# Weighing values on all four quarters of the array, with the output in two banks

## What is computed

```python
pos = jnp.arange(seq_len)
seg = pos // SEGMENT_LENGTH                      # 64
local = seg[None, :] == seg[:, None]
diff = jnp.abs(pos[None, :] - pos[:, None])
dil = (diff > 0) & (diff % 4 == 0) & (diff <= 256)
scores = jnp.einsum('bqhd,bkhd->bhqk', q, k) * scaling + mask[None, None]
attn = jax.nn.softmax(scores, axis=-1)
out = jnp.einsum('bhqk,bkhd->bqhd', attn, v).reshape(B, S, H * Dh)
return out @ w_o
```

## Time and profile before

| | before |
|---|---|
| device time, median of 3 | 471.31 us |
| span of the profiled execution | 468.8 us |
| PE busy | 444.4 us, 95% |
| DVE busy | 394.0 us, 84% |
| ACT busy | 333.3 us, 71% |
| POOL busy | 296.6 us, 63% |
| chain that ended last | PE 59%, POOL 9%, DMA 8%, DVE 8%, ACT 7% |

### The profile page before, as it was taken

How to read it: one execution, slowest core, us unless ns; L and a number is a source line. 1 busy time by engine, 2 the same in 40 slices (tenths; PEclk the granted TensorE clock), 3 DMA queues, 4 the chain that set the end, 5 groups by cost and what they waited for, 6 DMA issues and landing times.

```text
span 468.8 us, 17264 instructions
## 1 busy us (share of the span) xinstructions
PE 444.4 (95%) x6440; PEld 350.0 (75%) x6440; DVE 394.0 (84%) x1344; ACT 333.3 (71%) x975; POOL 296.6 (63%) x491
## 2 busy tenths in 40 slices
PE   7997899999999999999999999998987989999996
PEld 6685688888888888788887778887744757558775
DVE  6885798987888899889887698995899989998775
ACT  3686768868877877886786678695566579987533
POOL 4321488677666858667865588564669897674322
PEclk9999899999999999999999999999999999999999
DMA  7577852346335445344455565364000000000003
GB/s 224 183 246 209 247 142 52 73 99 133 80 74 112 76 79 105 76 85 94 98 108 124 112 124 108 75 125 91 1 1 0 0 2 1 1 0 2 1 0 91
DMA packets 136099, 40.53 MB, mean 86 GB/s; under 512 B 104977, under 2 KB 131025, under 8 KB 136017
## 3 DMA queue, kind: packets, MB, share of 16 engines
q1 hardware_dynamic: 135440, 38.38, 35.7%
q10 hardware_dynamic: 576, 1.05, 0.6%
HBM read 29.44 MB, written 9.96 MB: 84 GB/s over the span
## 4 chain that ended last, share of the span: by engine, by line
PE 59%; POOL 9%; DMA 8%; DVE 8%; ACT 7%; SPq 4%; issue 3%; ACTq 0%; POOLq 0%; DVEq 0%
PE psum L422 10%; PE psum L464 10%; PE psum L484 5%; PE psum L1186 5%; DMA w_rows_dram<-st 4%; PE psum L498 4%; PE psum L495 4%; PE psum L403 4%; PE psum L510 4%; PE psum L1181 3%; PE psum L405 3%; PE psum L404 3%; DMA st<-w_rows_dram 2%; POOL area L1827 2%; ACT pband L569 2%
## 5 line engine op out<-in xcount | busy, mean ns | idle before, releaser
L948 POOL TENSOR_SCALAR pband<-pband,fac 128x192 f32<-128x192 f32 x256 | 103.9, 424 | 80.6 <-DVE fac L771 80.4
L569 ACT ACTIVATE pband<-pband,st 128x192 f32<-128x192 f32 x256 | 113.1, 447 | 1.0 <-DVE st L719 1.0
L719 DVE CUSTOM_DVE_ANT_0 pband<-psum,band_mask 128x192 f32<-128x192 f32 x256 | 76.1, 353 | 0.1
L422 PE MATMUL psum<-keys,q_class 64*64 64x192 f32 (+2 forms) x1536 | 66.2, 274 | 0.0
L464 PEld LDWEIGHTS psum<-ident,pband 128*128 128x128 f32 x384 | 45.4, 141 | 21.4 <-issue 13.3
L422 PEld LDWEIGHTS psum<-keys,q_class 64*64 64x64 f32 x1536 | 57.6, 133 | 1.4 <-issue 1.4
L464 PE MATMUL psum<-ident,pband 128*128 128x128 f32 x384 | 53.0, 273 | 2.2 <-DVE pt L780 2.2
L569 ACT ACTIVATION_READ_ACCUMULATOR pband<-pband,st 128x1 f32 x256 | 49.3, 192 | 0.0
L938 POOL COPY q_class<-q_rows 128x512 f32<-128x512 f32 x32 | 36.5, 1142 | 19.2 <-ACT q_rows L609 19.2
L930 POOL COPY keys<-k_rows 128x512 f32<-128x512 f32 x32 | 36.1, 1130 | 14.0 <-ACT k_rows L601 7.1
L780 DVE COPY pt<-psum 128x512 f32<-128x512 f32 x64 | 43.7, 683 | 0.5
(11 more groups left out here) (213 smaller groups left out, 1090.7 us busy)
## 6 DMA issues: line engine op xcount, KB each, us to landing
v_rows_dram<-arena SPq DMA_DIRECT2D x32, 256.0 KB, 3.4
v_both<-v_rows_dram SPq DMA_DIRECT2D x32, 256.0 KB, 3.8
v_seg<-v_rows_dram SPq DMA_DIRECT2D x64, 128.0 KB, 3.6
v_side<-v_rows_dram SPq DMA_DIRECT2D x96, 64.0 KB, 2.6
w_rows_dram<-st SPq DMA_DIRECT2D x64, 8.0 KB, 3.0
st<-w_rows_dram SPq DMA_DIRECT2D x64, 8.0 KB, 2.5
arena<-_attn_hidden_states_dram SPq DMA_DIRECT2D x4, 256.0 KB, 3.7
out_dram<-x SPq DMA_DIRECT2D x4, 256.0 KB, 2.5
```

The lines of the kernel that those rows point to most:

```text
L422: return pe.matmul(bank[2 * r + head][rows, at:at + y.shape[1]], x, y, start=True, stop=True, skip_group_check=True)
L569: act.activation(x, x, ACT.Exp, bias=mine[:, head:head + 1], scale=-1.0, accum_out=mine[:, 2 + head:3 + head]).then_inc(s_exp, 1)
L719: dve.tensor_tensor_reduce(pband[:, G % P_SLOTS, c, head, :], bank[2 * r + head][:, at:at + BAND], band_mask[:, (0, 1, 1, 2)[w], SEG * (1 ...
L948: pool.tensor_scalar(x, x, fac[:, F % 2, 1, c, head:head + 1], 1.0, ALU.mult, ALU.mult).then_inc(s_scaled, 1)
```

## The change

Probabilities and values are laid out so that the two halves of the keys of a side or a segment product lie on the two halves of the partitions: a segment of the first 256 tokens of the window on partitions 0 to 63 and one of the last 256 on 64 to 127, side keys of an even class below and of an odd class above. Each head has its 64 columns, so a set of four products covers all four quarters. Quarters of different halves of the partitions write to different banks: the output of the first 256 tokens of a window goes to the first half of bank 6, that of the last 256 to the first half of bank 7. The side products are done in two parts (`weigh_sides(U, 0)` and `(U, 1)`), with the second scores' half between them. `weigh(U, 0)` and `(U, 1)` become 16 matmuls that are 64 wide. Queries are projected into bank 6, keys into bank 7, and `output` goes to the even transposes' bank. The loop's order changes on all engines, and so do the orders of prologue and tail; work beyond that is the same. The tail's functions change by one wait.

```diff
+HALF_SEGS = TW
+HALF_W = WT // 2
...
-        pseg = sb("pseg", [P, P_SLOTS, TW, 2, SEG])
-        pband = sb("pband", [P, P_SLOTS, DIL, 2, BAND])
+        pseg = sb("pseg", [P, P_SLOTS, 2, 2, 2, SEG])
+        pband = sb("pband", [P, P_SLOTS, 2, 2, 2, BAND])
         pt = sb("pt", [P, 2 * PT_SLOTS, 512])
         v_both = sb("v_both", [P, DIL, NW, P])
-        v_side = sb("v_side", [P, DIL, 2 * (NW - 1), DH])
-        v_seg = sb("v_seg", [P, T // SEG, DH])
+        v_side = sb("v_side", [P, 2, 2 * (NW - 1), P])
+        v_seg = sb("v_seg", [P, NW * HALF_SEGS, P])
...
+    s_sides, s_out, s_mix, s_acc = sem("s_sides"), sem("s_out"), sem("s_mix"), sem("s_acc")
...
-    turn_bank, out_bank, shared_bank = bank[4:6], bank[6], bank[7]
+    turn_bank, rows_bank, shared_bank = bank[4:6], bank[6], bank[7]
+    out_bank = [bank[6 + half][:, 0:HALF_W] for half in range(2)]
+    query_bank = [shared_bank, bank[6]]
...
-    for t in range(FIRST_STEP, NS_ALL + 8):
-        occupants += [(t - lag, who) for who, lag in (("key", 0), ("wo", 7), ("query", 0)) if there(t - lag)]
+    occupants += [(FIRST_STEP - 1, "query"), (FIRST_STEP, "key")]
     def wait_shared(pe, x, name):
+        if (x, name) not in occupants:
+            pe.wait_ge(s_out, x - FIRST_STEP + (name == "query"))
+            return
         at = occupants.index((x, name))
         if at:
             pe.wait_ge(*shared_reader(*occupants[at - 1]))
+    def band_of(G, c, head):
+        return pband[:, G % P_SLOTS, c // 2, head, c % 2, :]
+    def seg_of(G):
+        return pseg[:, G % P_SLOTS, :, :, :, :]
...
-                for head in range(2):
-                    sp.dma_start(v_seg[DH * head:DH * (head + 1), 2 * TW * w:2 * TW * (w + 1), :],
-                                 v_rows[WT * w:WT * (w + 1), P * p + DH * head:P * p + DH * (head + 1)].rearrange(
+                for half in range(2):
+                    sp.dma_start(v_seg[SEG * half:SEG * (half + 1), HALF_SEGS * w:HALF_SEGS * (w + 1), :],
+                                 v_rows[WT * w + HALF_W * half:WT * w + HALF_W * (half + 1), P * p:P * (p + 1)].rearrange(
                                      "(s x) f -> x s f", x=SEG)).then_inc(s_v[w], 16)
             def load_sides(p, w):
-                for head in range(2):
-                    for side in ((2 * w - 2, 2 * w - 1) if w else ()):
-                        sp.dma_start(v_side[DH * head:DH * (head + 1), :, side, :],
-                                     v_rows[DIL * SEG * (side + 1):DIL * SEG * (side + 2),
-                                            P * p + DH * head:P * p + DH * (head + 1)].rearrange(
-                                         "(x c) f -> x c f", c=DIL)).then_inc(s_v[w], 16)
+                for s in range(2 if w else 0):
+                    for odd in range(2):
+                        sp.dma_start(v_side[SEG * odd:SEG * (odd + 1), :, 2 * w - 2 + s, :],
+                                     v_rows[WT * w - HALF_W * (1 - s):WT * w + HALF_W * s, P * p:P * (p + 1)].rearrange(
+                                         "(x d o) f -> o x d f", d=2, o=2)[odd, :, :, :]).then_inc(s_v[w], 16)
...
+                to = shared_bank if kind else query_bank[t >= FIRST_STEP]
+                pe.matmul(to[:, :], hi, xn_hi[:, cols], start=True, stop=False)
+                pe.matmul(to[:, :], hi, xn_lo[:, cols], start=False, stop=False)
+                pe.matmul(to[:, :], lo, xn_hi[:, cols], start=False, stop=True).then_inc(s_proj[kind], 1)
...
+                    if c % 2 == 0:
+                        product(0, second, at, x0[:, second], y0[:, SEG:SEG + BAND])
+                        product(1, second, at, x1[:, second], y1[:, SEG:SEG + BAND])
+                        product(0, first, at, x0[:, first], y0[:, SEG:BAND])
+                        product(1, first, at, x1[:, first], y1[:, SEG:BAND])
+                        product(0, first, at + P, x0[:, first], y0[:, 0:SEG])
+                        product(1, first, at + P, x1[:, first], y1[:, 0:SEG])
...
+                        product(0, first, at, x0[:, first], y0[:, 0:BAND])
+                        product(1, first, at, x1[:, first], y1[:, 0:BAND])
...
+                if b == 0:
+                    wait(pe, s_acc, U - 1)
                 for k in range(4):
+                    i, head = divmod(k, 2)
                     if b < 2:
-                        src = pband[:, U % P_SLOTS, 2 * b + k // 2, k % 2, SEG * (k % 2):SEG * (k % 2) + P]
+                        src = band_of(U, 2 * b + i, head)[:, SEG * i:SEG * i + P]
                     elif b == 2:
-                        src = pband[:, U % P_SLOTS, k, :, :].rearrange("p h x -> p (h x)")[:, P:2 * P]
+                        src = pband[:, U % P_SLOTS, i, head, :, :].rearrange("p o x -> p (o x)")[:, P:2 * P]
                     else:
-                        src = pseg[:, U % P_SLOTS, k, :, :].rearrange("p h x -> p (h x)")
+                        src = pseg[:, U % P_SLOTS, i, head, :, :].rearrange("p i x -> p (i x)")
...
+            def turned(U, b):
+                odd, e = b % 2, 2 * U + b // 2
+                pe.wait_ge(s_pt[odd], e + 1)
+                return pt[:, PT_SLOTS * odd + e % PT_SLOTS, :]
+            def out_by_class(half):
+                return out_bank[half].rearrange("q (x c) -> q c x", c=DIL)
             def weigh(U, b):
                 if not there(U):
                     return
                 p, w = divmod(U, NW)
-                odd, e = b % 2, 2 * U + b // 2
                 if b == 0:
+                    pe.wait_ge(s_query, min(U + FIRST_STEP, NS_ALL))
+                    pe.wait_ge(s_key, min(U + FIRST_STEP + 1, NS_ALL))
                     wait(pe, s_out, U)
                     pe.wait_ge(s_v[w], (p + 1) * V_DMAS[w])
-                if b == 2 and w < NW - 1:
-                    pe.wait_ge(s_v[w + 1], (p + 1) * V_DMAS[w + 1])
-                pe.wait_ge(s_pt[odd], e + 1)
-                turned = pt[:, PT_SLOTS * odd + e % PT_SLOTS, :]
-                by_class = out_bank.rearrange("q (x c) -> q c x", c=DIL)
-                for k in range(4):
-                    if b < 2:
-                        c, head = 2 * b + k // 2, k % 2
-                        dims = slice(DH * head, DH * (head + 1))
-                        last = pe.matmul(by_class[dims, c, :], v_both[:, c, w, dims], turned[:, P * k:P * (k + 1)],
-                                         start=(b == 0 and k < 2), stop=False, skip_group_check=True)
-                        continue
+                mine = turned(U, b)
+                for i in range(2):
+                    c = 2 * b + i
                     for half in range(2):
-                        cols = slice(P * k + SEG * half, P * k + SEG * (half + 1))
-                        side = 2 * w + 1 if half else 2 * w - 2
-                        if b == 2 and not 0 <= side < 2 * (NW - 1):
-                            continue
                         for head in range(2):
                             dims = slice(DH * head, DH * (head + 1))
-                            if b == 2:
-                                last = pe.matmul(by_class[dims, k, SEG * half:SEG * (half + 1)], v_side[dims, k, side, :],
-                                                 turned[dims, cols], start=False, stop=False, skip_group_check=True)
-                            else:
-                                last = pe.matmul(out_bank[dims, cols], v_seg[dims, 2 * (TW * w + k) + half, :],
-                                                 turned[dims, cols], start=False, stop=(k == 3 and half == 1),
-                                                 skip_group_check=True)
-                last.then_inc(s_pv[odd], 1)
+                            at = P * (2 * i + head) + SEG * half
+                            last = pe.matmul(out_by_class(half)[dims, c, :], v_both[:, c, w, dims], mine[:, at:at + SEG],
+                                             start=(c == 0), stop=False, skip_group_check=True)
+                last.then_inc(s_pv[b], 1)
+            def weigh_segments(U):
+                if not there(U):
+                    return
+                w = U % NW
+                mine = turned(U, 3)
+                for j in range(2):
+                    for second in range(2):
+                        for head in range(2):
+                            for half in range(2):
+                                dims, mykeys = slice(DH * head, DH * (head + 1)), slice(SEG * half, SEG * (half + 1))
+                                cols, at = SEG * (2 * j + second), P * (2 * j + head) + SEG * second
+                                last = pe.matmul(out_bank[half][dims, cols:cols + SEG],
+                                                 v_seg[mykeys, HALF_SEGS * w + 2 * j + second, dims],
+                                                 mine[mykeys, at:at + SEG], start=False, stop=False, skip_group_check=True)
+                last.then_inc(s_pv[1], 1)
+            def weigh_sides(U, crossed):
```

(48 more changed lines are left out.)

255 lines of the change are left out of this document (125 added, 130 removed).

## The result

The changed kernel takes 492.19 us (median of 4 runs, 491.09 to 494.49) against 471.22 us for the kernel before on the same chip: a ratio of 1.045, 95% interval 1.041 to 1.049, slower. Its profiled execution has a span of 489.6 us, 20.8 more than 468.8. The forecast was 454.

The account below looks back on a forecast made before the run. PE was taken to bound the loop; 20.7 us saved, less 1.2 for quantising and 2.1 for statistics, took 17.4 off the 468.8 span: 451.4, plus 2.5 outside, 454 us. Its own case was 447 to 460, ends 446 and 464.

Parts of the forecast that it names:

- segments and sides: PE's weighing, two neighbours: 32 records each from 29 to 14.5 ns, saving 0.47 and 0.44 us a step.
- Band products: PE's weighing: 32 records 64 wide at 29 ns, 0.93 against 0.85 us, costing 0.08; entry 0.17.
- 25 ns floor: Rival: PE records adding into PSUM start no closer than 25 ns, so little is saved; 465.5 us, chance 0.08.
- dear narrow products: Rival: PE's 64-wide band products cost as much as wide ones, 64 ns a record; 480 us, chance 0.05.
- step lengths: PE-bound loop steps: 9.26 becomes 8.35 us with two neighbours, 8.79 becomes 8.32 with one.
- DVE's own work is 7.25 to 7.43 in a step without much quantising, under 8.32: VectorE in the loop: its 7.25 to 7.43 us of work would fit in the new step of 8.32.
- rival 2: Shared even bank makes PE wait for late DVE, 0.3 us a step, 9.6 over 32 steps; 463 us, chance 0.13.
- Quantising, 1.2 us: VectorE's quantising parts of about 1.0 us don't fit the slack: 0.2 us lost in each of six steps.
- Statistics, 2.1 us: Steps where DVE waits for statistics from DRAM keep their length: three steps' gain lost, bounds 0 and 5 us.
- the 2.45 that stay: Time already lost before the change in the two statistics steps of 10.60 and 10.37 us against 9.26.
- Prologue and tail, 0 with 4 either way: New instruction lists of prologue and tail: taken at no gain or cost, with 4 us either way.
- 2.7 us for the last six units: Gain in the last six outputs, woven into the tail: two thirds of 4.1 us because of PE's gaps.

Follow-up runs that it names:

- e1: Changed kernel with VectorE's two-operand subtraction `diff` replaced by a one-operand reduction, so the output is not the reference's; 481.26 us, ratio 1.021 to the kernel before.
- c4: Changed kernel with `diff` on GpSimd, former tail order behind each engine's last attention piece, and quantising spread over 21 steps; 471.20 us, ratio 0.999.
- c1: Changed kernel with `diff` moved to GpSimd and all tail functions in their former order; 488.02 us, ratio 1.026 to the kernel before.
- c2: c1 with the quantising spread over 21 steps in place of 15; 484.12 us, ratio 1.020 to the kernel before.
- c6: c4 with `output` between the next unit's segment and side products, and three woven pieces including `gu0(0)` moved forward; 478.71 us, ratio 1.013.
- t2: Changed kernel with tail functions in the former order only behind each engine's last attention piece; 490.69 us, ratio 1.032 to the kernel before.
- e2: Changed kernel with the subtraction `diff` moved from VectorE to GpSimd's queue, same result; 482.23 us, ratio 1.019 to the kernel before.
- e4: Changed kernel with `differences` behind the first `band_max` on VectorE and `exp_difference` between the first band exponentials' halves on ScalarE; 480.15 us, ratio 1.019.

## Why the prediction failed

Spans of the profiled executions, changed less before, in us:

| | forecast | measured |
|---|---|---|
| up to output 0 | -0.5 | -0.9 |
| output 0 to 25 | -14.2 (-17.5 + 1.2 + 2.1) | +9.5 |
| output 25 to the end | -2.7 | +12.2 |
| sum | -17.4 | +20.8 |

The loop missed by 23.7 us, of which e1 gives back 15.1; what lies behind output 25 missed by 14.9. None of the rivals had a time above 480.

**The segments and sides were right.** Where nothing disturbs, 32 segment records start 0.52 us ahead of the sides (c4: 99.43 to 99.95), against the 0.46 forecast and 0.93 before. In c4's timeline:

```profile
98.35 1.15 PE L516 MATMUL psum<-pt,v_both 128*64 128x64 f32 x32
99.43 0.69 PE L532 MATMUL psum<-pt,v_seg 64*64 64x64 f32 x32
99.95 0.29 PE L558 MATMUL psum<-pt,v_side 64*64 64x64 f32 x4
```

Band products took 1.08 from start to start (forecast 0.93 + 0.17 = 1.10). The rivals of the 25 ns floor and of dear narrow products are both out. The floor that the Trainium skill states ("TensorE: Matmul & The Clock Gate", section "Wait — 56ns, not 53.3ns?") would give an estimate of 0.80 for the 32 segment records; 0.52 disagrees with it.

**The step lengths were right where VectorE is on time.** In e1 the shortest step with two neighbours is 8.32 us (forecast 8.35), and one with one neighbour is 8.06 (forecast 8.32, too long by 0.26), both with PE busy throughout. Windows of e1:

```profile
176.72:185.04 8.32, 8.32 (x202) 6.80 (x201) 7.44 (x31) 6.92 (x24) 6.64 (x12) 1.00 0.43 87
97.76:105.82 8.06, 8.06 (x187) 6.80 (x185) 7.45 (x31) 6.96 (x24) 6.42 (x12) 1.00 0.39 85
```

Most steps of e1 are longer, 8.9 us on average up to output 25.

**The step that failed: "DVE's own work is 7.25 to 7.43 in a step without much quantising, under 8.32".** It took the durations of VectorE's instructions in the old order for those in the new one. VectorE's work was 8.9 to 9.8. The two windows were also among the lowest: over the 25 steps before, VectorE's work is 7.8 on average and above 8.1 in seven. In rows that the argument did not look at, `diff` already had 193 ns as its median and 1443 as its longest before the change: the price of a meeting with GpSimd stood in that trace. From output 0 to 251.64 us `diff` takes 32.2 us in 19 steps in the changed kernel, 1.5 us a step more than its shortest. VectorE needs about 7.4 + 1.5 = 8.9 without quantising and one more with it, and from the third on the steps are 8.8 to 10.3: DVE sets the step, not PE. This is rival 2's way, VectorE late at the even bank, and its sign is there (19.6 us of waits of L487), but not its size: without the meetings the loop to output 25 is 15.1 us shorter (237.1 in the changed kernel, 222.0 in e1), 0.6 us a step where the rival had 0.3. Over 32 steps that would be 19, an estimate, and more than the whole gain of 17.4. I sized it from DVE's busy time in the old order.

**Quantising, 1.2 us: too small.** Spreading it gained 3.3 us between output 0 and 28 (c1 to c2), though with `diff` on GpSimd. **Statistics, 2.1 us** beside the 2.45 that stay, 4.55 together: in c4 the two steps exceed undisturbed ones by 3.2 us (8.91 + 11.08 - 2 x 8.4), within the bounds.

**The loop's gain.** With these repaired, c4 goes from output 0 to 25 in 220.2 us, against 227.6 before and 213.4 by the forecast (227.6 - 17.5 + 1.2 + 2.1). TensorE's idle time in that stretch is 5.3 us behind VectorE's copies, 4.9 in pauses and 0.9 behind a copy of ScalarE's, 11.1 in all, where the kernel before had 1.9 and the forecast allowed 3.3 more. No term stood for the pauses, though the trace before had one, 1.1 us ahead of L498.

**Prologue and tail, 0 with 4 either way: wrong by more than its bound.** Behind output 25 the kernel loses 12.2 us where the forecast had a gain of 2.7. 5.0 lie ahead of `gu0` (43.5 from output 25 to `gu0` against 38.5): the steps up to the last output are 1.8 shorter (42.6 against 44.4), but `gu0` now stands 0.9 us behind the last `output`, where it stood 5.9 ahead of it (336.77 against 342.66). c6 shows that moving `gu0` alone doesn't mend this. 7.2 lie behind `gu0`. The former late lists win back 5.4, likely by shorter VectorE instructions; the 1.8 that they leave are put down to the lower clock just behind `gu0`, as read from t2's trace. The changed kernel had a stretch at the lower clock too, later, where TensorE had stood idle for 2.1 us ahead of products at 442.11:

```profile
438.00:446.00 8.00, 5.92 (x30) 4.77 (x29) 7.86 (x9) 4.70 (x17) 3.71 (x3) 0.82 0.01 2
```

It was 1.00 in the kernel before from 342 to 460 us. So the forecast's 2.7 us for the last six units shrank to 1.8, and the order of the lists spent them.

## What to carry to other kernels

An instruction's duration in a trace is a property of the order too. Before trusting it for a new order, look at its longest as well as its median: here the VectorE operation on two SBUF tiles that sometimes took seven times as long was one that had met GpSimd, and a change of order moves all such meetings. Give such an operation a single SBUF operand (as in e1), another engine (e2), or a place where GpSimd is idle (e4).

When TensorE's narrow products get faster, ask what feeds them besides data: pauses without a releaser that come every so many instructions, close behind a packet of the instruction queue, are waits for the program itself.

A list that leaves TensorE without filler work can cost it its clock: here idle stretches of 2.0 and 2.7 us came with 6.8 us at the lower level, and the 1.8 us that t2 kept.
